# One-head copies of queries and keys made by small DMAs into zeroed rings, moments kept twice, and vector work at other places in a decoder kernel

## What is computed

```python
x = x + attn(_layernorm(x))          # q, k, v: x @ W.T + b; top 32 of scores / sqrt(128); softmax; @ v; @ Wo.T + bo
x = x + xattn(_layernorm(x), ctx)    # 16 heads: softmax(Q K^T / sqrt(8)) V
x = x + ffn(_layernorm(x))           # expert = argmax(feats @ centroids.T); alpha = sigmoid(affinity)
# expert e: y = feats + relu((xhat*gamma + beta) @ w1 + b1) @ w2 + b2; out = alpha*y + (1-alpha)*feats
```

## Time and profile before

| | before |
|---|---|
| median of 3 runs | 467.24 us (464.86 to 468.54) |
| profiled execution, its own time | 466.77 us |
| its span | 465.0 us |
| busy: PE / DVE / POOL / ACT | 394.4 / 310.6 / 257.6 / 230.1 us |
| mean granted clock of PE | 0.948 of full speed |

### The profile page before, as it was taken

How to read it: one execution, slowest core, us unless ns; L and a number is a source line. 1 busy time by engine, 2 the same in 40 slices (tenths; PEclk the granted TensorE clock), 3 DMA queues, 4 the chain that set the end, 5 groups by cost and what they waited for, 6 DMA issues and landing times.

```text
span 465.0 us, 11829 instructions
## 1 busy us (share of the span) xinstructions
PE 394.4 (85%) x3737; PEld 271.7 (58%) x3738; DVE 310.6 (67%) x1222; ACT 230.1 (49%) x479; POOL 257.6 (55%) x363
## 2 busy tenths in 40 slices
PE   6688877889987985997998888887989799999990
PEld 6475634444543643554554444454569699988990
DVE  2568966697897894887788964666355156656660
ACT  1244524566565663665666562443410176666650
POOL 5846450333763696389387484682878134444441
PEclk9979987999999997998999997999998899999996
DMA  5100019201000001001000100010002533333320
GB/s 140 48 25 20 28 32 320 69 1 45 2 2 24 13 25 37 1 25 46 1 24 25 49 25 25 5 44 2 24 25 76 155 94 95 87 83 87 89 55 2
DMA packets 26311, 22.98 MB, mean 49 GB/s; under 512 B 3972, under 2 KB 23560, under 8 KB 26257
## 3 DMA queue, kind: packets, MB, share of 16 engines
q1 hardware_dynamic: 21600, 15.12, 11.7%
q0 software_dynamic: 2784, 6.37, 4.0%
q10 hardware_dynamic: 1872, 0.81, 0.8%
HBM read 14.73 MB, written 8.01 MB: 49 GB/s over the span
## 4 chain that ended last, share of the span: by engine, by line
PE 40%; DVE 22%; POOL 15%; issue 13%; ACT 5%; DMA 2%; SPq 1%; DVEq 1%; POOLq 0%; ACTq 0%
PE s_bank L1277 8%; DVE neg_hmax L831 6%; PE s_bank L358 6%; PE att_bank L369 4%; DVE self_room L823 4%; PE self_bank L369 3%; DVE best L817 3%; POOL rstd L577 2%; POOL routed_rows L668 2%; PE pvt_bank L1302 2%; PE cross_bank L1377 2%; ACT weights L1077 2%; PE s_bank L1246 2%; DVE stats L531 2%; PE self_bank L1241 2%
## 5 line engine op out<-in xcount | busy, mean ns | idle before, releaser
L831 DVE TENSOR_REDUCE neg_hmax<-s_bank 128x4 f32<-128x512 f32 x128 | 82.3, 684 | 49.0 <-PE s_bank L1266 48.8
L1077 ACT ACTIVATE weights<-s_bank 128x512 f32<-128x512 f32 x128 | 69.6, 595 | 70.9 <-PE s_bank L1282 70.9
L1266 PE MATMUL s_bank<-k_room,q_room 32*128 32x512 f32 x256 | 84.2, 670 | 2.1 <-DVE neg_hmax L831 2.1
L1277 PE MATMUL s_bank<-q_room,k_room 32*128 32x512 f32 x256 | 75.9, 670 | 1.0 <-POOL q_room L651 1.0
L434 POOL DMA_INDIRECT out<-x_in,q_room x39 | 37.8, 970 | 56.5 <-DVE x_in L398 50.7
L657 POOL TENSOR_TENSOR x<-x_bv,attended 128x128 f32<-128x128 f32 x32 | 14.6, 455 | 89.2 <-DVE attended L858 89.1
L1302 PE MATMUL pvt_bank<-weights,xv 128*32 128x128 f32 x1024 | 49.1, 286 | 8.9 <-ACT weights L1077 7.6
L384 DVE TENSOR_TENSOR q_room<-s_bank,b_cols 128x512 f32<-128x512 f32 x39 | 27.0, 692 | 33.5 <-PE s_bank L358 29.7
L1246 PE MATMUL s_bank<-ident 128*128 128x128 f32 x278 | 41.8, 310 | 4.0 <-POOL ident_bf L597 2.0
L1302 PEld LDWEIGHTS pvt_bank<-weights,xv 128*32 128x32 f32 x1024 | 21.3, 109 | 40.0 <-ACT weights L1077 37.1
L1246 PEld LDWEIGHTS s_bank<-ident 128*128 128x128 f32 x278 | 39.8, 225 | 7.3 <-issue 5.6
(11 more groups left out here) (173 smaller groups left out, 808.9 us busy)
## 6 DMA issues: line engine op xcount, KB each, us to landing
q_room<-routed_rows SPq DMA_DIRECT2D x39, 130.0 KB
w<-in_w SPq DMA_DIRECT2D x16, 256.0 KB, 5.8
x_in<-in_x SPq DMA_DIRECT2D x8, 256.0 KB, 3.0
ctx_in<-in_ctx SPq DMA_DIRECT2D x8, 256.0 KB
routed_rows<-blank SPq DMA_DIRECT2D x5, 130.0 KB
out<-x_in,q_room POOLq DMA_INDIRECT x39
routed_rows<-blank ACTq DMA_DIRECT2D x4, 130.0 KB
routed_rows<-pay,slot POOLq DMA_INDIRECT x32
```

The lines of the kernel that those rows point to most:

```text
L831: dve.tensor_reduce(neg_hmax[:, first:first + 4], bank.rearrange("p (h k) -> p h k", k=S), AX.X, ALU.max, negate=True).then_inc(s["s1_max" ...
L1077: act.activation(weights[:, u, :], s2_bank[:, (u % 2) * GS:(u % 2 + 1) * GS], ACT.Exp, scale=HEAD_SCALE).then_inc(s["s2_exp"], 1)
L1266: pe.matmul(s1_bank[:, (u % 2) * GS:(u % 2 + 1) * GS], natural(q_nat, g, j, strip(u)), masked(k_masked, K_RING, g, j, strip(u)), start=Tru ...
L1277: pe.matmul(s2_bank[:, (u % 2) * GS:(u % 2 + 1) * GS], natural(k_nat, g, j, u), masked(q_masked, Q_RING, g, j, u), start=True, stop=False)
```

## The change

- Masked copies of queries and keys are made by SP: `mask_queries` and `mask_keys` each issue 16 DMAs from SBUF to SBUF per group, one for each head, 8 partitions by 512 columns (16 KB). The rest of the rings is zeroed once by three memsets on DVE (128x4096 ahead of the first statistics, 128x4096 and 128x2048 before the first top-k). `head_mask`, POOL's four and ACT's four copies a group are gone.
- `moments` and `var_eps` are kept twice, by the parity of the group. Statistics wait for the moments of the group before instead of for POOL's subtraction. POOL's norm subtracts into the destination and multiplies in place; `centred` is gone.
- On DVE the first norm's statistics move from the start of the pass to behind those of the second norm; POOL's part moves from the end of the pass to behind the second norm. `choose` and alpha of a group move from the end of one pass to the first step of the next (`weigh`), except for the last two groups. The affinity copy stands between the two halves of top-k round 1.
- The value bias is no longer added by DVE: ACT copies the values out, and the bias is folded into `out_bias`, added with x once.
- POOL's slots and first scatter move behind the norms. ACT runs one small exponential ahead of all else. The experts' weights are loaded in four passes, four DMAs each, instead of sixteen in a row.

The core of the diff:

```diff
+            def spread_heads(dst, src, at0, done):
+                for head in range(H):
+                    first, block = head * HD, at0 + head % G * GS
+                    sp.dma_start(dst[first:first + HD, block:block + GS], src[first:first + HD, :]).then_inc(s[done], 16)
+            def mask_queries(g):
+                wait_alone(sp, s["xq_ready"], g + 1)
...
+                if later(g, Q_RING):
+                    wait_alone(sp, s["s2_done"], 16 * (g - Q_RING + 1))
+                spread_heads(q_masked, q_nat[:, (g % 3) * GS:(g % 3 + 1) * GS], (g % Q_RING) * MASKED, "xq_masked")
...
             def run(g):
                 has_f, has_c, has_e, has_s = stages(g)
                 load_later_x(g)
+                mask_queries(g + 1)
...
                     load_ctx(g + 3)
+                mask_keys(g + 2)
...
             dve.wait_ge(s[ready], count)
-            if not isinstance(g, int) or g >= 1:
-                dve.wait_ge(s[f"ln{n}_centred"], g)
+            if later(g, 1):
+                dve.wait_ge(s[f"ln{n}_moments"], G * g)
...
+            dve.memset(k_masked[:, 0:2 * MASKED], 0.0).then_inc(s["zeros_made"], 1)
             first_norm(0)
...
+                    dve.memset(q_masked, 0.0).then_inc(s["zeros_made"], 1)
+                    dve.memset(k_masked[:, 2 * MASKED:3 * MASKED], 0.0).then_inc(s["zeros_made"], 1)
...
                     normalise(f, 3)
+                if routed_later(f - 1):
+                    choose(dve, f - 1)
+                    weigh(f - 1)
...
                     norm_stats(dve, 1, x1, 0, e, "x1_ready", e + 1)
                     norm_moments(dve, 1, e)
+                if has_c and h + 1 < NG:
+                    first_norm(h + 1)
...
+            act.wait_ge(s["consts_made"], 3)
+            act.activation(aff_exp[:, :], minus_half[:, :], ACT.Exp)
...
-                    pe.wait_ge(s["xk_masked"], G * (g + 1))
+                    pe.wait_ge(s["xk_masked"], 16 * H * (g + 1))
...
-                    pe.wait_ge(s["xq_masked"], G * (g + 1))
+                    pe.wait_ge(s["xq_masked"], 16 * H * (g + 1))
```

More of the change, by code:

```diff
@@ L269, in routed_later @@
             return 0 <= f < NG - 2
-        def feats_count(f):
-            return f + G if last_group(f) else f + 1
         def later(g, first):
@@ L505, in run, with load_ffn @@
                     load_ctx(g + 3)
+                mask_keys(g + 2)
                 if isinstance(g, int) and g == NG - 3:
                     load_biases()
-            def load_ffn():
-                for e in range(E):
+            def load_ffn(experts):
+                for e in experts:
                     sp.dma_start(at(w1, e * F, F), T["w1"][e, :, :]).then_inc(s["ffn_loaded"], 16)
@@ L517, in _ @@
                 if g == 1:
-                    load_ffn()
                     wait_alone(sp, s["blank_made"], 2)
@@ L521, in _, with moments_of, var_eps_of @@
                 run(g)
+                if 0 <= g < E // 2:
+                    load_ffn((2 * g, 2 * g + 1))
             ffn_sync(sp)
+        normed = ("xn_ready", "xn2_ready", "feats_ready")
+        def moments_of(n, g, b):
+            return moments[n][:, half(g) * G + b, :]
+        def var_eps_of(n, g):
+            return var_eps[n][:, half(g) * G:(half(g) + 1) * G]
         def norm_stats(dve, n, src, base, g, ready, count):
             dve.wait_ge(s[ready], count)
-            if not isinstance(g, int) or g >= 1:
-                dve.wait_ge(s[f"ln{n}_centred"], g)
+            if later(g, 1):
+                dve.wait_ge(s[f"ln{n}_moments"], G * g)
             for b in range(G):
@@ L698, in run @@
                     add_attended(f, 3)
-                mask_queries(e - 1, 0)
-                if g < 0:
-                    for j in range(1, G):
-                        mask_queries(e - 1, j)
                 if has_e:
@@ L884, in read_counts, with weigh @@
                    .then_inc(s["counts_read"], 1)
+            def weigh(f):
+                dve.wait_ge(s["aff_exp_ready"], f + 1)
+                dve.tensor_scalar(aff_den[:, :], aff_exp[:, :], 1.0, None, ALU.add).then_inc(s["aff_den_ready"], 1)
+                dve.wait_ge(s["aff_den_ready"], f + 1)
+                if later(f, 2):
+                    dve.wait_ge(pay_stored[half(f)], 16 * G * (f // 2))
+                dve.reciprocal(pay_of(f)[:, :, ALPHA], aff_den[:, :]).then_inc(s["alpha_ready"], 1)
             def expert_bias(g, n):
@@ L903, in run @@
                        .then_inc(s["beta_made"], 1)
-                if not isinstance(g, int) or h + 1 < NG:
+                if not has_c and h + 1 < NG:
                     first_norm(h + 1)
@@ L995, in run @@
                     next_maxima(g, 2, 2)
-                if has_s:
-                    if not (isinstance(g, int) and g == -1):
-                        topk(h, 1)
-                    dve.wait_ge(s["v_done"], h + 1)
-                    if later(h, 2):
-                        dve.wait_ge(s["attn_done"], h - 1)
-                    dve.tensor_tensor(grouped(at(v, half(h) * GS, GS)), grouped(self_bank[:, :]),
-                                      spread(bvo_rows[:, :].rearrange("p (a n) -> p a n", a=1), [128, G, S]),
-                                      ALU.add).then_inc(s["v_ready"], 1)
+                if has_s and not (isinstance(g, int) and g == -1):
+                    topk_best(h, 1)
                 if has_f:
@@ L1011, in run @@
                        .then_inc(s["aff_ready"], 1)
+                if has_s and not (isinstance(g, int) and g == -1):
+                    topk_take(h, 1)
                 expert_bias(g, 2)
@@ L1181, in scores_out, with values_out @@
                         evacuate(scores[:, :], self_bank[:, :], "scores_done", h + 1, "scores_ready")
+                def values_out():
+                    if has_s:
+                        if later(h, 2):
+                            act.wait_ge(s["attn_done"], h - 1)
+                        evacuate(at(v, half(h) * GS, GS), self_bank[:, :], "v_done", h + 1, "v_ready")
                 def feats_out():
@@ L1219, in run @@
                 step(2, queries, probs_out)
-                step(3, lambda: masked_keys(0), self_keys)
+                step(3, nothing, self_keys)
                 step(4, scores_out, feats_out)
-                step(5, lambda: masked_keys(1), lambda: masked_keys(2))
-                step(6, lambda: masked_keys(3), xn2_out)
+                step(5, nothing, values_out)
+                step(6, nothing, xn2_out)
                 step(7, affinity_exp, cross_queries)
```

155 lines of the change are left out of this document (58 added, 97 removed).

## The result

The changed kernel took 466.34 us (median of 20; 459.18 to 469.83) where the kernel before, on the same chip, took 468.07 (median of 20): 1.7 us less, 0.996 by the medians. The recorded ratio is 0.991, 95% interval 0.988 to 0.994. On another chip it was 466.53 against 467.46, 0.998 by the medians, 0.996 (0.993 to 1.000) as a recorded ratio. The forecast was 446.5. So 1 to 4 us are gained of the 20.8 forecast. The profiled execution took 466.39 us, its span 464.6, against 466.77 and 465.0.

What follows compares the result with a forecast made beforehand. PE was taken to bound the cross-attention stretch, so only its waits and lost clock could be won: 14.6 + 5.4 + 2.8 + 1.0 - 1.5 - 1.5 + 0 = 20.8 us off 466.77, median 446.5, range 438 to 457.

Steps and rivals of the forecast that it cites:

- The border, 14.6 us: Starts of passes 0 to 6: moving DVE's statistics and choice from ahead of the maxima cuts PE's waits by 14.6 us.
- The clock, 5.4 us: Rounds behind three border stalls return to 8.13 us at full clock, saving 2.15, 1.61 and 1.64 us.
- The third part: Round behind the last of the three stalls, a wait of 0.85 us: 1.64 us saved by full clock.
- a granted clock near 1.0 between 100 and 270 us: Sign named in advance that would show the forecast right, in the cross-attention passes.
- Affinity copy, 2.8 us: PE's four waits for the affinity copy shrink by 0.7 us each as DVE reaches it earlier; bounds 0 and 3.6.
- Masks, 1.0 us: PE's wait for POOL's masked query copy goes, 1.0 us; SP's 32 extra DMAs a pass cost nothing.
- the 20 that I had named as a sign: Sign named in advance: SP's mask issues near 0.45 us each, finished within 20 us of a pass.
- the third rival: SP cannot keep up with 32 more DMA issues a pass and slows the kernel, to 509 us in its example; 4%.
- What comes in, -3 us: Statistics and choice at new places delay maxima of the fifth and second steps, 1.5 us lost for each.
- the first rival: DVE is late elsewhere: choice and statistics each make maxima 1 us late in their passes; 457 us, 12%.
- The fill, 0 with bounds of 1.5: Ahead of the passes: DVE's three memsets balance against an earlier table load and removed work; 0, bounds -1.5 and +1.5.
- Last groups, 0: Behind the passes: the experts' loop unchanged and the last two groups routing as before, so 0.

Runs made afterwards that it cites:

- the second: The changed kernel profiled once more, without any edit, beside the kernel before on another chip; 0.996 of the kernel before, 0.998 by the medians.
- the filled kernels: Two versions of the kernel before with useless products on PE where it waits at the borders, many or fewer; 1.004 and 0.998 by the medians.
- moves_only: The changed kernel with one-head copies made by POOL and ACT as before, without mask DMAs or DVE memsets; 0.993 of the kernel before.
- before_reduce: The kernel before with only the cast and subtraction of the maxima written as three reductions; 1.003 of the kernel before.
- filled: The kernel before with 10, 4, 20, 40, 14 and 8 useless PE products at the borders of passes 0 to 5; 1.005 of the kernel before.
- reduce_only: The changed kernel with neg_max on ACT, epsilon on POOL, and the maxima's cast and subtraction as three reductions; 0.975 of the kernel before.
- all_three: The changed kernel with reductions for blocked small instructions, later memsets, and POOL's last scalings of w behind the scatters; 448.05 us, 0.962 of the kernel before.
- filled_less: The kernel before with useless PE products at the borders cut to the stalls' length (3, 2, 11, 21, 8, 4); median 466.38 us against 467.31.

## Why the prediction was wrong, point by point

The step that failed first is that of the border: DVE's instructions were moved forward at the durations that they had had behind the wait. Two more terms were put at nothing and cost 9.4 us in the profiled pair.

1. *The border, 14.6 us.* The direction was right, the size not: passes 0, 1, 2 and 5 have no wait left, passes 3, 4 and 6 still have 1.99, 1.98 and 1.19. The failed step is "What stands behind comes forward by that much, and no further than until PE no longer waits". It took DVE's durations from rows in which these instructions did not meet POOL; moved forward, `neg_max` was blocked for 2.92 us. 10.6 of the 15.8 us at the borders were won.
2. *The clock, 5.4 us.* The rounds behind the borders of passes 3 and 4 came down to 8.12 and 8.13 us, and the filled kernels bear the mechanism out for them. The third part, 1.64 us behind the border of pass 6, did not come: that round takes 10.03 us (274.49 to 284.52), with a low stretch from 275.7 to 282.5 behind a wait of 1.19. And I let the clock change only there. Low clock fell by 11 us in the loop, rose by 7.5 ahead of it and by 12 between the last transpose and the routed rows. The sentence "a granted clock near 1.0 between 100 and 270 us" held in the first profile and not in the second, where it is low from 179.1 to 182.6 and from 240.6 to 247.4; I had not asked about the rest.
3. *Affinity copy, 2.8 us.* Its wait is gone (3.6 us).
4. *Masks, 1.0 us.* The wait is gone. The DMAs' issue was mis-sized: 16 take 11.49 us, 0.72 each for my 0.48, so 23 us of a pass for 15, and not the 20 that I had named as a sign:

```profile
23.36 11.49 SPq L496 DMA_DIRECT2D k_room<-k_room  x16
```

   No engine waits for them; the third rival is refuted, and its point from which it decides, 1.1 us, was not reached.
5. *What comes in, -3 us.* Here the first rival (12%) came true in one of its two steps. The third round waits 1.03 us in passes 0 to 3 and 0.81 in pass 4, where it waited 0 to 0.76, so in the five passes that I named, but for a reason beside the 1.27 us of statistics: `var_eps` blocked by POOL for another 0.86. The choice, on the other hand, now starts unblocked (L587: 0.18 us median for the 0.886 of the earlier trace rows). The Trainium skill's rule that I weighed there was of two-input instructions, and I applied it to the choice alone; what cost most, `neg_max`, `var_eps` and the cast, has one tensor input. The rival had 12% and stood at 457.
6. *The fill, 0 with bounds of 1.5.* It lost 3.5 us: by differences of single profiles 2.2 for memsets and DMAs and 3.2 for the clock, less 1.9 that the moves give back there (moves_only 75.03 against before_reduce 76.89, both with the long low stretch). My price for a memset was right, and "just fits before x lands" was wrong by 0.8 us.
7. *Last groups, 0.* It lost 5.9 us. I wrote "The experts' loop is as it was, and the last two groups route as before" and did not ask what POOL has queued when the loop ends: scatters and scalings that used to lie earlier, 2 to 3 us. The clock cost the other half.

Sum in the profiled pair: -10.1 in the loop, +3.5, +5.9 and +0.3, so -0.4 us for -20.8. The forecast had all of its 20.8 in the loop. What I can count there is 5.0 us of waits for the maxima, 4.6 for affinities and masks, and an estimated 3.9 of clock, 13.5 in all; why PE's rounds take back the 3.4 us between that and 10.1 is open.

## What to carry to other kernels

A small instruction moved next to another engine's long ones must be priced at its blocked duration, not at its usual one: look in the timeline of both engines at the moment it will run, and see which of its kind are ever long. If the critical path goes through it, write it in a form that no trace shows blocked (here a reduction), and look again afterwards: the block fell on the next scalar operation, which cost over a microsecond in two passes. And when a stall is taken out of a loop, follow the engine queues to the loop's end: work that was hidden in the stall comes out there.

## What the runs showed of the hardware

- One DVE instruction, 0.17 us when alone, took 2.92 us across a scatter (1.00), an addition (1.29) and a product (1.05) of POOL, each begun less than 0.1 us after the one before had ended, and ended with the third.
- Reductions from SBUF to SBUF stayed at 0.170 to 0.172 us (32 of them) where a cast of the same 128x16 elements reached 2.18.
- Executions of one program differ by 1 to 2% with the mean granted clock, in most kernels about 3 us per 0.01; two kernels within 1% should be compared with their clocks beside the times.
- In the loop, a microsecond at the low clock cost 0.35 to 0.36 us (two pairs of profiles).
- The kernels whose loop had no PE wait over 1.04 us had 0 to 3.4 us of low clock in it, the others 10.4 to 26.8. Median clocks of 0.968 (filled), 0.958 (reduce_only) and 0.973 (all_three) stand against 0.950 before, but filled_less is at 0.954.
